# A selective scan block: VectorE's C products in place in SBUF, whole and one unit later

## What is computed

```python
xz = x @ W_in.T
xc, z = jnp.split(xz, 2, axis=-1)          # 1024 channels each
xc = silu(causal_conv4(xc))
dbc = xc @ W_xproj.T                       # 32 + 16 + 16 columns
delta = jax.nn.softplus(dlt @ W_dt.T + b_dt)
A = -jnp.exp(A_log)                        # 1024 x 16
def step(h, inp):                          # over the 8192 rows
    dA, dBx, c = inp                       # exp(delta*A), delta*B*xc, C
    h = dA * h + dBx
    return (h, jnp.einsum('bdn,bn->bd', h, c))
y = (ys + xc * D) * silu(z)
return y @ W_out.T
```

## Time and profile before

| | |
|---|---|
| median of 3 runs | 5145.01 us (5144.02 to 5146.02) |
| the profiled execution's own time | 5143.12 us |
| its span, first to last instruction | 5141.0 us |
| mean granted clock of TensorE | 0.975 of full |
| DVE, PE, POOL, ACT busy, share of the span | 93%, 93%, 75%, 65% |

### The profile page before, as it was taken

One profiled execution on the slowest core, in us unless ns is written; L12 is line 12 of the kernel. 1 busy time (PEld: TensorE's weight loads), 2 busy tenths in 40 slices (PEclk: granted clock), 3 DMA queues, 4 the chain that ended last, 5 costly groups with the idle time before them and its releaser, 6 DMA issues. The chain is left out here.

```text
span 5141.0 us, 67238 instructions
## 1 busy us (share of the span) xinstructions
PE 4760.4 (93%) x21964; PEld 3282.7 (64%) x21964; DVE 4789.6 (93%) x5476; ACT 3335.7 (65%) x7037; POOL 3830.8 (75%) x1722
## 2 busy tenths in 40 slices
PE   8799899998999989989899899967999999999999
PEld 3455555555555555555555555555888888888888
DVE  8999999999999999999999999997888888888887
ACT  3777877778777787777777877765444444444442
POOL 6999999999999999999999999994322322322231
PEclk9899999999999999999999999988999999999999
DMA  7555565555656556556565666554010011001100
GB/s 259 181 194 195 192 203 184 198 194 189 200 186 200 194 187 205 187 198 197 188 198 188 194 200 189 186 173 156 25 38 31 31 34 36 31 31 37 31 31 29
DMA packets 402675, 745.79 MB, mean 145 GB/s; under 512 B 44083, under 2 KB 44211, under 8 KB 402198
## 3 DMA queue, kind: packets, MB, share of 16 engines
q1 hardware_dynamic: 401590, 738.08, 43.6%
q0 software_dynamic: 736, 3.41, 0.2%
HBM read 698.05 MB, written 43.26 MB: 144 GB/s over the span
## 5 line engine op out<-in xcount | busy, mean ns | idle before, releaser
L712 POOL TENSOR_TENSOR slot<-du,b_row 128x1024 f32<-128x1024 f32 x1024 | 2393.5, 2369 | 1.5 <-DMA b_row<-b_c_rows 1.4
L1045 DVE TENSOR_TENSOR_SCAN decays<-decays,state,slot 128x512 f32<-128x512 f32 x1376 | 1687.4, 1271 | 60.6 <-POOL slot L712 54.8
L912 ACT ACTIVATE decays<-delta,rate 128x512 f32<-128x512 f32 x2048 | 1385.2, 687 | 50.6 <-DVE slot L993 2.2
L1106 PE MATMUL work_ps<-h_t,win 128*128 128x512 f32 x2048 | 982.2, 627 | 137.7 <-ACT delta L848 109.2
L1183 PEld LDWEIGHTS y_ps<-ident,slot 128*128 128x128 f32 x8192 | 944.9, 143 | 238.3 <-issue 177.7
L1183 PE MATMUL y_ps<-ident,slot 128*128 128x128 f32 x8192 | 1019.5, 277 | 42.8 <-POOL slot L719 29.2
L1569 POOL TENSOR_TENSOR hq<-hid,qinv 128x1408 f32<-128x1408 f32 x63 | 163.4, 2594 | 1001.7 <-DVE qinv L1595 1001.7
L1052 DVE TENSOR_TENSOR slot<-decays,c_row 128x512 f32<-128x512 f32 x1376 | 871.5, 674 | 1.8 <-DMA c_row<-b_c_rows 1.8
L719 POOL TENSOR_TENSOR slot<-slot,c_row 128x1024 f32<-128x1024 f32 x336 | 794.6, 2365 | 81.6 <-ACT state L901 79.6
L1045 DVE TENSOR_TENSOR_SCAN slot<-decays,state,slot 128x512 f32<-128x512 f32 x672 | 819.4, 1264 | 2.8 <-POOL slot L712 2.2
L1106 PEld LDWEIGHTS work_ps<-h_t,win 128*128 128x128 f32 x2048 | 393.8, 201 | 590.1 <-issue 493.3
(11 more groups left out here) (274 smaller groups left out, 7358.0 us busy)
## 6 DMA issues: line engine op xcount, KB each, us to landing
b_row<-b_c_rows SPq DMA_DIRECT2D x1024, 256.0 KB, 3.9
c_row<-b_c_rows SPq DMA_DIRECT2D x1024, 256.0 KB, 3.7
win<-in_w_in SPq DMA_DIRECT2D x256, 256.0 KB, 4.4
xt<-in_x SPq DMA_DIRECT2D x16, 1024.0 KB, 7.0
xr<-in_x SPq DMA_DIRECT2D x64, 256.0 KB, 4.3
x_after_mamba<-xr SPq DMA_DIRECT2D x64, 256.0 KB, 4.6
xa<-x_after_mamba SPq DMA_DIRECT2D x64, 256.0 KB, 2.9
xres<-x_after_mamba SPq DMA_DIRECT2D x64, 256.0 KB, 2.6
```

The source lines that it names most:

```text
L712: pool.tensor_tensor(slot[:, u % SLOTS, :, :], du[:, p % 2, :, :], two(b_row[:, u % BC_RING, :]), ALU.mult).then_inc(S["ub_ready"], 1)
L912: act.activation(decay[u % 2][:, i, :], delta[:, p % 2, i, :], ACT.Exp, scale=rate[:, 2 * p + i, n:n + 1]).then_inc(S["decay_ready"], 1)
L1045: dve.tensor_tensor_scan(d if u in DVE_C else h, d, h, state[:, 2 * p + i, n:n + 1], ALU.mult, ALU.add).then_inc(S["scan_done"], 1)
L1106: op = pe.matmul(dst[:, :], win[:, i % WIN_RING, k, :], h_t[:, k, :], start=(k == 0), stop=(k == KT - 1))
```

## The change

1. All scans write their slot, none the decays.
2. DVE's C product reads and writes the slot in place, one instruction of 2 x 512 columns in the place of two of 512 (the form that POOL's has). It stands one unit later: behind the scans of u + 1. It waits for the state copy of u, and for `c_row`.
3. ACT copies the state of every unit from the slot, both columns at once, when both scans are done. The semaphore `half_used` is gone.
4. `decays(u)` waits for the scan of u - 2 with the same i, for every u.
5. `DVE_C` has 47 units instead of 43; the 17 that POOL keeps are 3, 6, 8, 16, 21, 23, 28, 30, 32, 36, 39, 46, 49, 50, 53, 56 and 62.
6. The tables are placed anew: `BANK`, and all five tables of steps. Each has the same pieces as before, most of them within three positions of their old place. The largest moves: the four `xd` of blocks 2 to 5 four to nine positions earlier, one load of x rows seven and the first load of weights five later, one save sixteen later and another six earlier, two squares of the norm three and five later.

The diff, with most of the tables left out:

```diff
 DVE_STEPS = {
-    (4, 0): [("gate", 6, -1)], (5, 1): [("gate", 7, -1)], (21, 0): [("gate", 0, 0)], (32, 0): [("gate", 1, 0)],
-    (36, 1): [("gate", 2, 0)], (49, 1): [("gate", 3, 0)], (51, 1): [("gate", 4, 0)], (53, 0): [("gate", 5, 0)],
+    (4, 0): [("gate", 6, -1)], (5, 0): [("gate", 7, -1)], (21, 0): [("gate", 0, 0)], (33, 0): [("gate", 1, 0)],
+    (36, 0): [("gate", 2, 0)], (49, 0): [("gate", 3, 0)], (51, 0): [("gate", 4, 0)], (51, 1): [("gate", 5, 0)],
     (56, 0): [("x_low", 0, 1)],
 }
 POOL_STEPS = {
-    6: [("du", 1, 0)], 13: [("newton", 0, 1)], 21: [("du", 2, 0)], 46: [("du", 3, 0)], 60: [("du", 0, 1)],
+    4: [("du", 1, 0)], 13: [("newton", 0, 1)], 21: [("du", 2, 0)], 44: [("du", 3, 0)], 61: [("du", 0, 1)],
...
 SP_STEPS = {
-    0: [("load_xr", 3, -1), ("load_win", 14, 0)], 1: [("load_xr", 2, -1)], 6: [("load_win", 15, 0)],
...
+    0: [("load_win", 13, 0), ("load_win", 14, 0)], 2: [("load_xr", 3, -1), ("load_win", 15, 0)],
...
-    2, 3, 4, 6, 8, 9, 11, 12, 14, 15, 16, 19, 20, 21, 22, 24, 26, 27, 29, 30, 31, 34, 35, 36, 38, 39, 41, 42, 43, 44,
-    45, 47, 48, 51, 52, 53, 55, 57, 58, 59, 60, 61, 63,
+    0, 1, 2, 4, 5, 7, 9, 10, 11, 12, 13, 14, 15, 17, 18, 19, 20, 22, 24, 25, 26, 27, 29, 31, 33, 34, 35, 37, 38, 40, 41,
+    42, 43, 44, 45, 47, 48, 51, 52, 54, 55, 57, 58, 59, 60, 61, 63,
...
@@ -516,10 +517,6 @@
                 first = {(k, a): s for k, a, s, _ in ITEMS}
                 order.sort(key=lambda ka: -first[ka])
                 return {BANK[ka]: ka for ka in order}
-
-            def half_used(u, c):
-
-                return c.at(len(DVE_C), sum(v <= u for v in DVE_C))

             def c_done(u, c):

@@ -893,10 +890,7 @@

                     def save_state(u, i, c):
                         p, n = divmod(u, N)
-                        if u in DVE_C:
-                            wait(act, *((S["half_used"], half_used(u, c)) if i == 0 else c_done(u, c)))
-                            act.activation(state[:, 2 * p + i, n:n + 1], decay[u % 2][:, i, T - 1:T], ACT.Copy).then_inc(S["state_saved"], 1)
-                        elif i == 0:
+                        if i == 0:
                             wait(act, S["scan_done"], c.at(2 * UNITS, 2 * u + 2))
                             act.activation(state[:, 2 * p:2 * p + 2, n], slot[:, u % SLOTS, :, T - 1], ACT.Copy).then_inc(S["state_saved"], 2)

@@ -907,8 +901,8 @@
                             act.wait_ge(prep_rounded, len(PREP))
                         if n == 0:
                             wait(act, *piece_read("d", 2 * p + i, c))
-                        if exists(cc) and v in DVE_C:
-                            wait(act, S["state_saved"], c.at(2 * UNITS, 2 * (u - 2) + i + 1))
+                        if exists(cc):
+                            wait(act, S["scan_done"], cc.at(2 * UNITS, 2 * v + i + 1))
                         act.activation(decay[u % 2][:, i, :], delta[:, p % 2, i, :], ACT.Exp,
                                        scale=rate[:, 2 * p + i, n:n + 1]).then_inc(S["decay_ready"], 1)

@@ -1042,18 +1036,13 @@
                         if i == 0:
                             wait(dve, S["ub_ready"], c.at(UNITS, u + 1))
                         d, h = decay[u % 2][:, i, :], slot[:, u % SLOTS, i, :]
-                        dve.tensor_tensor_scan(d if u in DVE_C else h, d, h, state[:, 2 * p + i, n:n + 1],
-                                               ALU.mult, ALU.add).then_inc(S["scan_done"], 1)
-
-                    def times_c(u, i, c):
-                        if i == 0:
-                            wait(dve, *ring_loaded(c_loaded, c, u))
-                        wait(dve, S["scan_done"], c.at(2 * UNITS, 2 * u + i + 1))
-                        op = dve.tensor_tensor(slot[:, u % SLOTS, i, :], decay[u % 2][:, i, :], c_row[:, u % BC_RING, :], ALU.mult)
-                        if i == 0:
-                            op.then_inc(S["half_used"], 1)
-                        else:
-                            op.then_inc(c_row_used[u % BC_RING], 1)
+                        dve.tensor_tensor_scan(h, d, h, state[:, 2 * p + i, n:n + 1], ALU.mult, ALU.add).then_inc(S["scan_done"], 1)
+
+                    def times_c(u, c):
+                        h = slot[:, u % SLOTS, :, :]
+                        wait(dve, S["state_saved"], c.at(2 * UNITS, 2 * u + 2))
+                        wait(dve, *ring_loaded(c_loaded, c, u))
+                        dve.tensor_tensor(h, h, two(c_row[:, u % BC_RING, :]), ALU.mult).then_inc(c_row_used[u % BC_RING], 1)

                     def body(c):
                         for pos in range(UNITS):
@@ -1064,9 +1053,9 @@
                                 HAVE[step](arg, cc)
                                 if cc.reg is None and cc.off == 0:
                                     prep_between(step, arg)
-                            if exists(c) and pos in DVE_C:
-                                times_c(pos, 0, c)
-                                times_c(pos, 1, c)
+                            v, cc = back(c, pos - 1)
+                            if exists(cc) and v in DVE_C:
+                                times_c(v, cc)
                             for step, arg, cc in steps(DVE_STEPS, c, (pos, 1)):
                                 HAVE[step](arg, cc)
                                 if cc.reg is None and cc.off == 0:
```

More of the change, by code:

```diff
@@ L44 @@
     0: [("z", 4, 0), ("d", 2, 0)], 1: [("d", 3, 0)], 2: [("z", 5, 0), ("y", 6, -1)], 3: [("y", 7, -1)],
[11 rows of a table removed]
[11 rows of a table added]
 }
 ACT_STEPS = {
[L58 to L71, removed]
@@ L72 @@
-    58: [("softplus", 0, 1)], 61: [("z_out", 1, 1)], 62: [("xd", 1, 1), ("z_out", 2, 1)], 63: [("xd", 0, 1)],
+    1: [("ln_sum", 1, 1)], 2: [("ln_sum", 2, 1), ("z_out", 4, 0)],
+    3: [("softplus", 1, 0), ("y_out", 6, -1), ("y_out", 7, -1), ("ln_sum", 3, 1)], 4: [("ln_square", 0, 1)],
+    5: [("xd", 3, 0)], 7: [("xd", 2, 0), ("z_out", 5, 0)], 8: [("z_out", 6, 0)], 10: [("ln_square", 1, 1)],
+    11: [("residual", 0, -1)], 12: [("ln_square", 2, 1), ("ln_square", 3, 1)], 13: [("seed", 0, 1)],
@@ new lines @@
+    14: [("z_out", 7, 0)], 15: [("residual", 1, -1)], 16: [("softplus", 2, 0)], 17: [("ln_apply", 0, 1)],
+    18: [("ln_apply", 1, 1), ("ln_apply", 2, 1), ("y_out", 1, 0)],
+    20: [("residual", 2, -1), ("ln_apply", 3, 1), ("y_out", 0, 0)], 21: [("silu_z", 0, 0)],
+    24: [("xd", 4, 0), ("h_out", 2, 1)], 25: [("h_out", 1, 1), ("xd", 5, 0), ("residual", 3, -1)],
+    26: [("h_out", 0, 1), ("h_out", 3, 1)], 27: [("in_out", 0, 1)], 28: [("in_out", 1, 1)], 32: [("conv_out", 0, 1)],
+    34: [("in_out", 2, 1), ("conv_out", 1, 1)], 35: [("y_out", 2, 0)], 36: [("y_out", 3, 0)],
@@ new lines @@
+    37: [("in_out", 3, 1), ("conv_out", 2, 1)], 38: [("in_out", 4, 1)], 39: [("softplus", 3, 0)],
+    41: [("conv_out", 3, 1)], 44: [("in_out", 5, 1)], 45: [("in_out", 6, 1)], 46: [("conv_out", 4, 1), ("xd", 6, 0)],
+    48: [("conv_out", 5, 1)], 49: [("conv_out", 6, 1), ("in_out", 7, 1), ("xd", 7, 0)],
+    51: [("y_out", 5, 0), ("y_out", 4, 0)], 52: [("conv_out", 7, 1)], 53: [("silu_x", 0, 1)], 55: [("z_out", 0, 1)],
+    57: [("x_out", 0, 1)], 58: [("softplus", 0, 1)], 59: [("ln_sum", 0, 2), ("z_out", 1, 1)], 60: [("xd", 0, 1)],
@@ L73 @@
+    62: [("z_out", 2, 1), ("z_out", 3, 1)], 63: [("xd", 1, 1)],
 }
 DVE_STEPS = {
-    (4, 0): [("gate", 6, -1)], (5, 1): [("gate", 7, -1)], (21, 0): [("gate", 0, 0)], (32, 0): [("gate", 1, 0)],
-    (36, 1): [("gate", 2, 0)], (49, 1): [("gate", 3, 0)], (51, 1): [("gate", 4, 0)], (53, 0): [("gate", 5, 0)],
+    (4, 0): [("gate", 6, -1)], (5, 0): [("gate", 7, -1)], (21, 0): [("gate", 0, 0)], (33, 0): [("gate", 1, 0)],
+    (36, 0): [("gate", 2, 0)], (49, 0): [("gate", 3, 0)], (51, 0): [("gate", 4, 0)], (51, 1): [("gate", 5, 0)],
@@ L83 @@
 SP_STEPS = {
-    0: [("load_xr", 3, -1), ("load_win", 14, 0)], 1: [("load_xr", 2, -1)], 6: [("load_win", 15, 0)],
-    11: [("load_xr", 1, -1)], 14: [("load_win", 0, 1), ("save_x1", 0, -1)], 18: [("load_xr", 0, 0)],
-    23: [("load_win", 1, 1)], 27: [("load_win", 2, 1)], 30: [("load_win", 3, 1)], 32: [("save_x1", 2, -1)],
-    34: [("load_win", 4, 1), ("save_x1", 1, -1)], 42: [("load_win", 5, 1)], 43: [("load_win", 6, 1)],
-    46: [("load_win", 7, 1)], 47: [("load_win", 8, 1)], 50: [("save_x1", 3, -1)],
-    52: [("load_win", 9, 1), ("load_win", 10, 1), ("load_win", 11, 1)], 56: [("load_x", 0, 2)], 60: [("save_bc", 0, 1)],
-    61: [("load_win", 12, 1)], 63: [("load_win", 13, 1)],
+    0: [("load_win", 13, 0), ("load_win", 14, 0)], 2: [("load_xr", 3, -1), ("load_win", 15, 0)],
+    4: [("load_xr", 2, -1)], 11: [("load_xr", 1, -1)], 17: [("save_x1", 0, -1)], 19: [("load_win", 0, 1)],
+    24: [("load_win", 1, 1)], 25: [("load_xr", 0, 0)], 28: [("load_win", 2, 1)], 29: [("load_win", 3, 1)],
+    33: [("load_win", 4, 1), ("save_x1", 2, -1)], 40: [("load_win", 5, 1)],
+    43: [("load_win", 6, 1), ("load_win", 7, 1)], 44: [("save_x1", 3, -1)], 46: [("load_win", 8, 1)],
```

(8 more changed lines are left out.)

## The result

The changed kernel takes **6089.69 us** (median of 4 runs), the kernel before 5144.52 beside it: a ratio of 1.184, 95% interval 1.183 to 1.186, 945 us slower. Forecast were 5967 us and 5650 to 6250.

The account below looks back on a forecast made before the run. DVE and POOL together were taken to bound the scan stage at 212.6 us a chunk. A chunk of 264 adds 51.4, x 16 = 822, to 5143.1, and 1.9 for the median gives 5967 us, range 5650 to 6250.

Parts of the forecast that it names:

- (d): Scan stage: DVE's product with two SBUF inputs and POOL's products take strict turns; POOL loses 1.01 us per meeting.
- its least: Scan stage, DVE never waiting: POOL needs 198.0 + 47 x 1.01 = 245.5 us a chunk.
- I take 264, between chance and locked phase: Scan stage: chosen chunk time of 264 us, between 259.5 for random meetings and 267.8 for a fixed rhythm.
- the locked pattern: Scan stage: DVE repeatedly asks just after POOL starts, written out between POOL's own units; 267.8 us a chunk with gates.
- Ahead by a hair: After a DVE product, POOL starts its next at 2.24 us, just before DVE's scans end at about 2.28.
- (b): DVE's C product as one 1024-element instruction, both inputs in SBUF: 1225 ns alone, 1.14 us start to start against 1.18.
- (e): DVE's product one unit later, waiting for ACT's state copy: nothing, between -1 and +3 us a chunk.
- (g): Matmuls, evacuations, gates, du products and loads placed anew: nothing, between -1 and +2 us a chunk.
- The first rival: No turns between DVE and POOL in the scan stage: 5132 us, or 5190 if idle time stays; chance 0.08.
- The second rival: POOL doesn't hand over between queued products, DVE waits until POOL runs dry: 320 us a chunk, 6860 us; chance 0.06.
- The third: DVE wins the turns, POOL is the bound at 245.5 us a chunk: 5671 us, the forecast's lower end, no separate chance.
- (f): ACT's state copies, 107 become 64, 18.0 to 13.1 us; ACT is busy 77%, so nothing gained.

Follow-up runs that it names:

- run 1: The changed kernel with DVE's product multiplying the slot by the next unit's decays (PSUM) instead of c_row (SBUF), ACT's decays also waiting for it: 5267.6 us.
- run 8: The kernel before, with DVE's product as one 1024-column instruction from decays (PSUM) and c_row into the slot, behind its own scans: 5220.2 us.
- run 3: The changed kernel with DVE's product issued as two halves of 512 columns in the same place: 6593.4 us.
- run 7: The changed kernel with every scan cut by 96, 32 or 16 of 512 columns, three versions: 5648.1, 5670.8 and 5895.4 us.
- run 6: The kernel before's tables and 43 units with the changed code, DVE's product reading the next unit's decays (PSUM) in place of c_row: 5236.4 us.
- 4: The changed kernel's instructions with the tables, banks and list of 43 units of the kernel before: 5963.7 us.
- run 2: The changed kernel with DVE's product moved from behind the two scans of the next unit to between them: 6326.9 us.

## Why the prediction was right, and where its terms were off

**The step that carried it held.** DVE's product with two SBUF inputs and POOL's products exclude each other (d). Three kinds of product stood beside POOL's: from slot and decays (run 1) and from decays and `c_row` (run 8), one input in PSUM each, and none of them waited; from slot and `c_row`, both in SBUF, most did. So it is neither the slot nor the broadcast row by itself, and run 3 shows the turns a second time. The figures of a meeting were right to some hundredths: a waiting product is done 1.08 us after POOL's end (1.09 foretold), POOL's 2.21 us after DVE's (2.24). By these POOL loses 0.97 us a meeting and not 1.01, and its least is 198.0 + 47 x 0.97 = 243.6 a chunk and not 245.5, which fits the 244.2 and 245.6 us of run 7 with 1.1 and 2.0 us of POOL's idle time in them.

**The step that was mis-sized is "I take 264, between chance and locked phase".** Measured 271.7. The phase does lock, and the locked pattern gave 267.8. Its waits were 267.8 - 157.1 - 53.6 = 57.1, against 59.3 measured: 2.2 more. DVE's idle time in the stage, for which the sum had none, adds 3.2 a chunk; the product's own 1.0 and some tenths in the scans go off again. That the pattern came so near is in part luck. Between two of POOL's own units it gave 11.4 us where they are three apart, and the trace has 11.4 at the median of 70; but for two apart it gave 8.0 against 7.0 in the mean, for four 17.1 against 19.1, for five 20.5 against 21.9, and these errors offset each other in part. "Ahead by a hair" was the right reading, and the hair is 0.10 to 0.20 us.

**(b), the product by itself**: 1.19 us and 1.12 from start to start, foretold 1.225 and 1.14; 1 us a chunk.

**(e) and (g), "nothing"**, hold in the changed kernel, where DVE idles 3.2 us a chunk against 4.3 before. They don't hold where nothing meets: run 6 has 114 us behind the state copy, run 1 has 78 us there and 52 of the gates behind PE, and the tables alone cost 242 us with the old code. That the meetings cover these waits in the changed kernel is an inference from these runs. The first rival, "no turns", gave 5132 us; runs 1 and 6, without turns, took 5268 and 5236, so as far as they show the change loses even where nothing meets, though part of that is a wait of their own.

**The second rival**, no hand-over between queued products, is false as a rule: a free turn passes to DVE between products of POOL that overlap by 0.04 us. It held once in the changed kernel, as told below. The third, DVE wins its turns, is what 32 columns less come near to.

**(f)**: ACT is busy 57% of the middle of the stage instead of 77%, and no time that bounds the kernel came of it.

## What to carry to other kernels

Before an operand moves from PSUM to SBUF, look whether VectorE then reads two SBUF tensors while GpSimd works: here a 1.19 us product paid 1.26 us of waiting in the mean, and splitting it made it worse. Where two engines take turns, the time depends on who asks first, so compare the start of one's next instruction with the request of the other to hundredths of a us; 0.13 us of work per unit decided over 419 - 133 = 286 us here. An instruction that waits in such a turn is booked as busy: only its duration against the shortest of its kind shows it.

## What was not expected

**DVE passed over five times.** In the first chunk one product took 11.55 us. DVE's timeline, then POOL's:

```profile
135.81 2.46 DVE L1039 TENSOR_TENSOR_SCAN slot<-decays,state,slot 128x512 f32<-128x512 f32 x2 [2.31 <-POOL slot L709]
142.58 11.55 DVE L1045 TENSOR_TENSOR slot<-slot,c_row 128x1024 f32<-128x1024 f32 x1 [4.32 <-ACT state L895]
154.05 4.79 DVE L1039 TENSOR_TENSOR_SCAN slot<-decays,state,slot 128x512 f32<-128x512 f32 x4
```

```profile
138.55 0.59 POOL L312 DMA_DIRECT2D down_quantised<-slot  x1 [0.30 <-POOL slot L680]
139.17 2.35 POOL L709 TENSOR_TENSOR slot<-du,b_row 128x1024 f32<-128x1024 f32 x1
141.47 2.35 POOL L656 TENSOR_TENSOR du<-delta,xc 128x1024 f32<-128x1024 f32 x1
143.78 2.35 POOL L709 TENSOR_TENSOR slot<-du,b_row 128x1024 f32<-128x1024 f32 x1
146.10 2.35 POOL L716 TENSOR_TENSOR slot<-slot,c_row 128x1024 f32<-128x1024 f32 x1
148.42 4.62 POOL L709 TENSOR_TENSOR slot<-du,b_row 128x1024 f32<-128x1024 f32 x2
158.58 2.34 POOL L709 TENSOR_TENSOR slot<-du,b_row 128x1024 f32<-128x1024 f32 x1 [5.54 <-DMA b_row<-b_c_rows]
```

It asked at 142.58 and was served when POOL ran dry at 153.04, at the fifth end. It is the first product of DVE's to start after POOL had itself issued a transfer (138.55). The runs 3, 4 and the three of 7 have one such case too, of 11.0 to 12.1 us, and run 2 has one of 4.4 us that was passed over once and served when POOL ran dry. In each it stands in the same place, 1.2 to 4.6 us behind the start of the same transfer. In the changed kernel no other product took over 3.4 us, and each of them was served at the next end. That the transfer is the cause is not shown; it stays open.

**PE's clock.** The mean granted clock in the scans fell from 0.98 to 0.90 while PE's busy share fell from 92% to 79%, with 354.1 us of its waits behind DVE's product. A summing matmul went from 277 to 301 ns in the mean. In run 1 the clock is 0.98 again, with PE busy 89%, and the matmul takes 282 ns. PE had room, and no wait that these runs show on the path is put down to its clock.

**The scan** costs 2.03 ns a column, the product 1.04: scans are 151.7 of DVE's 207.8 us a chunk in the kernel before, and that, not the product, is where a cut would count.
